# One step's token stage moved ahead of its projections and scores, on all engines

## The reference

```python
h = tok(x)                                   # 256 rows -> 128 rows
h = h + attn(layernorm(h))
h = h + ffn(layernorm(h))
```

```python
q = (xv @ Wq.T + bq) / sqrt(192)             # 8 queries to a group
k, v = split(xv @ Wkv.T + [0, bkv])          # 8 keys, 8 values
attn = softmax(q . k over the 192 features)  # 8 x 8 in each group
out = q.T + attn @ v.T                       # 8 rows of 192 to a group
```

## Time and profile before

| | us |
|---|---|
| median of 3 runs | 932.97 (932.45 to 934.08) |
| the profiled execution, its own time | 933.01 |
| its span, first to last instruction | 931.1 |
| PE busy in the span | 916.6 (98%) |
| DVE, ACT, POOL busy | 758.6, 654.8, 658.8 |
| mean granted TensorE clock | 0.998 |

### The profile page before, as it was taken

How to read it: one execution, slowest core, us unless ns; L and a number is a source line. 1 busy time by engine, 2 the same in 40 slices (tenths; PEclk the granted TensorE clock), 3 DMA queues, 4 the chain that set the end, 5 groups by cost and what they waited for, 6 DMA issues and landing times.

```text
span 931.1 us, 26765 instructions
## 1 busy us (share of the span) xinstructions
PE 916.6 (98%) x7762; PEld 811.4 (87%) x7762; DVE 758.6 (81%) x2000; ACT 654.8 (70%) x2496; POOL 658.8 (71%) x970
## 2 busy tenths in 40 slices
PE   8999999999999999999999999999999999999988
PEld 5778989888999888899988899988889988889867
DVE  4788888888889888888888888988888888888843
ACT  3457777777777777777777777777777777777753
POOL 2787767777777777777777777777877677777750
PEclk9999999999999999999999999999999999999999
DMA  6155554455554445554445555444556444555330
GB/s 208 36 154 139 158 142 123 129 139 155 144 158 127 125 126 151 144 166 133 124 131 144 146 152 152 124 127 130 155 144 165 133 119 129 150 143 157 111 111 18
DMA packets 195776, 126.20 MB, mean 136 GB/s; under 512 B 31152, under 2 KB 187184, under 8 KB 195760
## 3 DMA queue, kind: packets, MB, share of 16 engines
q1 hardware_dynamic: 192880, 122.59, 47.7%
q10 hardware_dynamic: 2880, 3.41, 1.1%
HBM read 70.11 MB, written 55.84 MB: 135 GB/s over the span
## 4 chain that ended last, share of the span: by engine, by line
PE 91%; DMA 3%; DVE 3%; POOL 1%; issue 1%; SPq 1%; ACT 0%; ACTq 0%; DVEq 0%; POOLq 0%
PE ring L891 15%; PE ring L1086 14%; PE bank L910 12%; PE ring L929 10%; PE ring L958 5%; PE ring L991 5%; PE bank L958 5%; PE ring L867 4%; PE ring L997 3%; PE ring L1016 3%; PE bank L991 2%; PE ring L1047 2%; PE ring L1037 2%; PE ring L1028 2%; PE bank L997 2%; PE ring L1012 1%
## 5 line engine op out<-in xcount | busy, mean ns | idle before, releaser
L327 ACT ACTIVATE E<-ring,m_neg 128x128 f32<-128x128 f32 x768 | 270.9, 372 | 38.6 <-DVE m_neg L620 38.6
L491 POOL TENSOR_TENSOR E<-E,e_rcp 128x512 f32<-128x512 f32 x160 | 166.2, 1040 | 97.1 <-DVE e_rcp L643 94.7
L483 POOL TENSOR_TENSOR qkT<-rot_c,rot_s 128x256 f32<-128x256 f32 x256 | 186.9, 730 | 20.1
L481 POOL TENSOR_TENSOR rot_s<-rot_s,rope_qs 128x256 f32<-128x256 f32 x192 | 142.2, 741 | 31.7 <-DVE rot_s L614 31.7
L327 ACT ACTIVATION_READ_ACCUMULATOR E<-ring,m_neg 128x1 f32 x768 | 162.2, 211 | 0.0
L620 DVE TENSOR_REDUCE m_neg<-ring 128x4 f32<-128x512 f32 x192 | 127.6, 679 | 18.7 <-PE ring L929 18.7
L1086 PE MATMUL ring<-wo_sb,OT 128*128 128x192 f32 x756 | 139.7, 335 | 0.0
L910 PE MATMUL bank<-wout_sb,G 128*128 128x192 f32 x744 | 135.8, 326 | 0.0
L634 DVE STREAM_TRANSPOSE EB<-E 128x512 f32<-128x512 f32 x189 | 131.0, 696 | 1.0 <-POOL E L491 1.0
L1086 PEld LDWEIGHTS ring<-wo_sb,OT 128*128 128x128 f32 x756 | 121.1, 190 | 7.9 <-issue 0.4
L910 PEld LDWEIGHTS bank<-wout_sb,G 128*128 128x128 f32 x744 | 120.4, 190 | 0.0
(11 more groups left out here) (155 smaller groups left out, 2330.6 us busy)
## 6 DMA issues: line engine op xcount, KB each, us to landing
spill<-EB SPq DMA_DIRECT2D x189, 256.0 KB, 2.4
ET<-spill SPq DMA_DIRECT2D x252, 128.0 KB, 2.7
ET<-spill SPq DMA_DIRECT2D x252, 64.0 KB, 2.4
x_sb<-in_x_dram SPq DMA_DIRECT2D x64, 192.0 KB, 2.5
out_dram<-out_sb SPq DMA_DIRECT2D x31, 192.0 KB, 2.1
x_sb<-in_x_dram SPq DMA_DIRECT2D x64, 64.0 KB, 2.3
w_raw<-in_w_att_dram ACTq DMA_DIRECT2D x2, 608.0 KB, 4.7
win_raw<-in_w_in_dram ACTq DMA_DIRECT2D x2, 384.0 KB, 6.1
```

The lines of the kernel that those rows point to most:

```text
L327: last = nc.scalar.activation(E[:, a, s * P:(s + 1) * P], RING[a][:, s * P:(s + 1) * P], ACT.Exp, bias=m_neg[:, a, s:s + 1], accum_out=e_s ...
L481: nc.gpsimd.tensor_tensor(rot_s[:, b, :, a], rot_s[:, b, :, a], sin, ALU.mult).then_inc(sin_out, 1)
L483: nc.gpsimd.tensor_tensor(qkT[:, b, :, a], rot_c[:, b, :, a], rot_s[:, b, :, a], ALU.add).then_inc(q_out, 1)
L491: nc.gpsimd.tensor_tensor(e, e, r, ALU.mult).then_inc(prob_out, 1)
```

## The change

It acts only in step 0 (`early`, and `first == "att"` on PE). Nothing is computed anew. PE's list is written out apart: `tok_qk`, projections 0 and 1, `tok_scores`, projections 2 and 3 and the values, `tok_mix`, one filler, `tok_h`, `scores(0)`, four fillers, `scores(1)`, two fillers, `x_turned`. Two waits of PE change: `tok_h` waits for all four rotations and not for the first exps, and `scores(0)` waits for the new h (`h_out`). DVE takes `token_qk` first, `token_max` between the second and third rotation, `tok_mixed` before the first maxima, and `h_stats` behind the last maxima of half 0 and the first inverse. ACT takes `token_exp` first, and `residual_kept` and `h_added` ahead of the score exps. POOL takes `token_bias` and `rstd1` between the rotations of half 0 and half 1.

```diff
--- before.py
+++ after.py
@@ -408,14 +408,20 @@
                     gelus()
                 if att and ffn:
                     v_kept_late()
+                early = isinstance(p, int) and p == 0
+                if early:
+                    token_exp()
                 if att:
                     bias_summed()
                     v_out_of_psum()
+                if early:
+                    residual_kept()
+                    h_added()
                 if att and fin:
                     exp_warmed()
                 if att and ffn:
                     heads_out(p - 1, LATE_HEADS[0])
-                if tok:
+                if tok and not early:
                     token_exp()
                 if starts:
                     act.wait_ge(s_w2, 16 * 2)
@@ -424,8 +430,9 @@
                 if att:
                     score_exp(0, 0)
                     score_exp(0, 1)
+                if att and not early:
                     residual_kept()
-                if tok:
+                if tok and not early:
                     h_added()
                 if att:
                     score_exp(0, 2)
@@ -509,12 +516,16 @@
                     nc.gpsimd.tensor_copy(h2_kept[:], h2[:]).then_inc(h2_copied, 1)
 
                 starts = isinstance(p, int) and p == -1
+                early = isinstance(p, int) and p == 0
                 if att:
                     need(pool, sc_mm, 6 * p)
                     for a in range(2):
                         for i in range(4):
                             rotated(a, i, 4 * a + i + 1)
-                if tok:
+                        if early and a == 0:
+                            token_bias()
+                            rstd1()
+                if tok and not early:
                     token_bias()
                 if starts:
                     wait_apart(pool, pool_passed, (bias_out, 1), (s_hi, 2))
@@ -768,22 +779,30 @@
                     dve.wait_ge(h2_out, done)
                     nc.vector.bn_stats(st2[:, a, :], h2[:, a, :]).then_inc(ln2_st, 1)
 
+                early = isinstance(p, int) and p == 0
+                if early:
+                    token_qk()
                 if att:
                     rotate(0)
                     rotate(1)
                 if att and ffn:
                     blocks_turned(1, 2, p - 1)
+                if early:
+                    token_max()
                 if att:
                     rotate(2)
                     rotate(3)
-                if tok:
+                if tok and not early:
                     token_qk()
                     token_max()
-                if att:
+                if att and not early:
                     key_max(0, (0, 1))
                 if tok:
                     token_probs()
                     tok_turned()
+                if early:
+                    tok_mixed()
+                    key_max(0, (0, 1))
                 if att:
                     key_max(0, (2,))
                     sums_inverted(0, 0, p)
@@ -791,8 +810,10 @@
                     dve.wait_ge(h_kept[0], p)
                     need(dve, h2_copied, p - 1)
                     attention_added(0, 2 * p - 1, late=True)
-                if tok:
+                if tok and not early:
                     tok_mixed()
+                if early:
+                    h_stats()
                 if starts:
                     attention_lo()
                 if att:
@@ -917,6 +938,8 @@
                     pe.wait_ge(q_out, 8 * p + 4 * a + 4)
                     if a == 0:
                         pe.wait_ge(v_out, p + 1)
+                        if first == "att":
+                            pe.wait_ge(h_out, n + 1)
                     else:
                         need(pe, h2_out, 2 * p - 1)
                         if tok:
@@ -1039,7 +1062,9 @@
                     last.then_inc(m_mm, 1)
 
                 def tok_h():
-                    if att:
+                    if first == "att":
+                        pe.wait_ge(rot_out, 4 * p + 4)
+                    elif att:
                         pe.wait_ge(exp_out, 6 * p + 1)
                     pe.wait_ge(m_out, n + 1)
                     for a in range(2):
@@ -1094,6 +1119,23 @@
                 if first == "att":
                     pe.wait_ge(s_lo, 1)
                     pe.wait_ge(s_low, 1)
+                if first == "att":
+                    tok_qk()
+                    qk_projected(0)
+                    qk_projected(1)
+                    tok_scores()
+                    qk_projected(2)
+                    qk_projected(3)
+                    v_projected()
+                    tok_mix()
+                    kept_warm(1)
+                    tok_h()
+                    scores(0)
+                    kept_warm(4)
+                    scores(1)
+                    kept_warm(2)
+                    x_turned()
+                    return
                 if att:
                     qk_projected(0)
                     qk_projected(1)
@@ -1107,7 +1149,7 @@
                     v_projected()
                 if tok:
                     tok_qk()
-                if first in ("tok", "att"):
+                if first == "tok":
                     kept_warm(2)
                 if fin:
                     ffn_second(0, p - 2, range(1))
@@ -1121,8 +1163,6 @@
                 if att and ffn:
                     output(0, p - 1, late=True)
                 if first == "tok":
-                    kept_warm(3)
-                if first == "att":
                     kept_warm(3)
                 if tok:
                     tok_mix()
@@ -1140,13 +1180,11 @@
                     scores(1)
                 if att and ffn:
                     output(1, p - 1, late=True)
-                if first == "att":
-                    kept_warm(4)
                 if fin:
                     ffn_second(0, p - 2, range(1, 3))
                 if tok:
                     x_turned()
-                if first in ("tok", "att"):
+                if first == "tok":
                     kept_warm(1)
                 if first == "ffn":
                     kept_warm(3)
```

## The result

The changed kernel takes 942.09 us (median of 4 runs, 940.58 to 942.73) beside 933.46 of the kernel before on the same chip: the ratio is 1.0094, 95% interval 1.0082 to 1.0106. It is slower by 8.6, forecast were 9. Its profiled execution took 941.50 with a span of 939.5; that of before took 933.01, so the two traces differ by 8.5. All lines of the kernel shift by a few to some twenty numbers: L998 are the fillers (L975 before), L952 the scores (L929), L912 the projections (L891), L488 and L490 POOL's rotation (L481, L483), L631 the maxima (L620), L604 and L606 xn (L593, L595), L623 a rotation's first operation (L612).

A forecast was written before the change was run, and what follows sets the result against it. PE was taken to bound the loop (busy 28.00 of 28 us), so a step-0 delay passes whole; step 0 itself is not PE-bound. 7.25 + 1.0 + 0.4 + 0.6 = 9.25 on 933.0 gives 942 us, range 938.5 to 946.

The forecast's parts named there:

- The mechanism: Step 0, POOL: rstd1 waits for DVE's late h statistics, so half 1's rotations and scores(1) come 8.3 us later.
- the mark: Start of DVE's first rotation of step 1: 48.88 before, forecast 56.1 without clock terms, 7.25 us later.
- 1.14 + 8.47: Full-clock times: scores(1) start to DVE's first maximum of half 1, then to DVE's first rotation of step 1.
- the half clock's first term: scores(1) on PE would run at half clock after a stall of 7.6 us: +1.0 us.
- The 0.4 for a fall behind the first stall: scores(0) could run at half clock after PE's 1.9 us stall ahead of tok_mix: +1.0 at four in ten.
- The 0.6 for fillers that hold x_turned: Half-clock fillers ahead of x_turned and step 1's second projections could delay DVE by 0 to 1.4 + 2.7; 0.6 taken.
- The sum: Whole run: 7.25 for the later first rotation of step 1, plus 1.0, 0.4 and 0.6 for the clock: +9.25 us.
- The xn term: First xn on DVE: shift 6.5 if DVE goes first, 7.25 if the port lock only moves to the other engine.
- (a): Step 0, POOL: the hold costs nothing because statistics come in time; -0.4, so 932.6 us; chance 4%.
- (b): Step 0: the early h moves its dependents along, first rotation of step 1 at 44.6, time 928.7 us; chance 3%.
- (c): Step 1: its PE fillers give way and swallow 2.74, leaving +4.5, so 937.5 us; chance 7%.
- (d): Same POOL hold, clock low throughout both scores and the fillers behind: +12.3, so 945.3 us; within the main case's 86%.

The follow-up runs named there:

- POOL's part alone: The kernel before with only POOL's token_bias and rstd1 moved between the rotations of half 0 and half 1: 941.85 us, ratio 1.0101.
- the fillers experiment: The changed kernel with 15 fillers instead of 4 ahead of scores(1): 938.81 us, ratio 1.0069.
- the one with the end fillers: The changed kernel with three more fillers near the end of the run, ahead of the last pair's attention product: 941.20 us, ratio 1.0083.
- the put-back kernel: The changed kernel with POOL's old list: token_bias behind all eight rotations, rstd1 behind the first softmax product: 932.32 us, ratio 1.0005.
- two ahead: The changed kernel with POOL's rstd1 behind the second of half 1's four rotations instead of ahead of the first: 938.03 us, ratio 1.0060.
- early norm: The changed kernel with h_stats behind tok_mixed, x_normalised before half 1's maxima, rstd1 then token_bias after half 1's rotations, x_hi earlier, no fillers behind scores(1): 932.83 us.
- the last version: The changed kernel with h_stats and x_normalised early, rstd1 behind half 1's second rotation, five fillers before scores(1), one behind x_turned, three near the end: 931.54 us, ratio 0.9982.

## Why the prediction was right

**The mechanism** was as forecast. PE, DVE and ACT with the new order and POOL with the old one give the old time; POOL's part alone gives the new one.

**The times along the chain**, forecast and measured: projections from 22.95, 22.54; scores(0) 34.6, 34.05; rs done 40.4, 40.06; half 1's rotations done 46.45, 46.00; scores(1) 46.5, 46.06. I was some 0.5 late from h on (it is written at 33.91, forecast 34.55). tok_qk starts at 21.28 and not at 21.6, but that is not the cause: the chain to h runs over DVE from the end of FL, as I had taken it. In this trace FL is 0.15 earlier, `token_qk` and `token_max` took 0.2 less than I gave them, and from the inverse to the turned weights it is 1.0 and not 1.3 (the t_a product took 0.57 and not 0.77).

**From scores(1) to the mark** I had 1.14 + 8.47 = 9.6 at full clock and 10.6 with the half clock's first term; it is 10.74. Of the clock's three parts, the 1.0 on the scores was right (0.9 by the maximum, 1.1 by the fillers experiment). The 0.4 for a fall behind the first stall did not come: that stall was 1.37 and the clock is 1.00 there. The 0.6 for fillers that hold x_turned is 0.1 to 0.2 in the profiled execution (x_turned at 50.79, xn done at 50.68; DVE waited 0.16) and 0.5 in the one with the end fillers. So the clock's cost varies from run to run. The longer runs of the changed kernel have the lower clocks, but these 0.5 are not enough for the whole spread from 940.6 to 942.7; the rest of it stays open.

**The sum** was 9.25. Measured are 7.92 at the mark: 0.5 less by the earlier h, and 0.85 less by the two clock terms that were too large. At the end it is 8.5. From the mark to the span's end there are 882.2 to 882.7 in the four traces with the clock's fall near the end, those of before and changed among them, and 881.0 to 881.9 in the eight without; the 0.5 is within that spread, and no experiment explains it. The median is a further 0.6 above the profiled run, and the median of the kernel before 0.45 above its own. So it is luck that the forecast of 942.0 comes this near to 942.09: the terms were 1.3 too large at the mark, some 0.7 that I did not have in the sum came behind it or between runs, and the base was 0.45 above the 933.0 that I had added to.

**The xn term** went as the larger value said. DVE was first, as I had thought possible (0.35 at 48.87), and the next xn operation then took 1.03 beside POOL's product (49.14): from the first to the end of the fourth it is 1.81 there and was 1.82. The port rule that I had cited from the Trainium skill, "SBUF — State Buffer", section "SBUF: two separate sides", agrees with this trace in its second form: the wait was only moved. The trace shows the durations (0.35, then 1.03 beside a product of 1.09) and not the lock itself.

**The rivals.** (a), no cost of POOL's hold, is what the put-back kernel shows it would have been: 932.3. (b) failed for the reason given. (c) failed: step 1's fillers (54.88 to 57.6) lie beside DVE's chain, and the third projection waited 0.54 behind them for the rotation, as before. (d) is not seen in any run.

## What to carry to other kernels

An engine that takes its work in order must not be given a wait ahead of work that others need and that is ready: four rotations of 1.5 each stood for 7 us behind a 1.3 us job whose input came late in another engine's list. To move a stage ahead on all engines, move each of its steps only as far as its input is ready there, and read for each new wait how long its producer's list is. A long stall of PE can cost the half clock behind it on top of its own length (1.1 at the mark behind 7.63), while stalls of 1.37 in the changed kernel and of 1.36 with POOL put back had a clock of 1.00 behind them, and the latter cost nothing. Fillers in the long stall were cheap. Fillers behind it were not: two of them, partly or wholly at half clock, took 2.0 to 2.6 where they took 1.56 with POOL put back, and held x_turned.

## What the runs showed of the hardware

- Nearly the same idle stretch has the clock fall behind it in one execution and not in another. The wait of PE near the end (1.80 to 1.95) was followed by half clock for some 3 us in the traces of the kernel before, of the changed one, of POOL put back and of two ahead, and by none in the other four that have it. A part of the spread of runs of one kernel is this: with the kernel before on one chip, six runs at a mean clock of 0.998 lie from 933.0 to 933.3, and 21 at 1.000 from 931.7 to 932.9.
- The four `x_normalised` operations of DVE, from SBUF to SBUF, take 0.30 to 0.37 each with no POOL product beside them. Beside one, an operation took up to 1.14, and in three orders (changed kernel 1.03, early norm 1.02, the last version 1.14) one of the four always paid it.
